# Token embedding, sink attention and soft mixture of experts on one core: two powers in place of four in GpSimd's scale chain

## The chip, the cores and the metric

The kernel runs on one core of a Trainium2 chip. The metric is the device time of one execution in microseconds (us), as the median of several runs; lower is better. An engine is named by its short name in the profile: PE is TensorE (matmul), PEld its weight load, DVE VectorE, ACT ScalarE, POOL GpSimd, SP SyncE. L1104 is line 1104 of the kernel.

## What is computed

For 64 images (3 x 224 x 224) and 64 texts (128 tokens of width 192):

```python
h = tokenize(x)                      # 196 patches per image, layernorm over 3840 values, times W
h = concat([h, txt], axis=1)         # 324 tokens of width 192
h = h + attention(layernorm(h))      # 12 heads, causal, rotary, one sink logit a head, softmax
h = h + experts(layernorm(h))        # soft mixture of 64 slots
```

The part that the change touches is the head of `experts`. Its input is the second layernorm of h; a root-mean-square norm follows, then a norm to unit length, and the product with the slots gives the logits:

```python
def _layernorm(x):  return (x - m) / jnp.sqrt(v + 1e-5)
xn  = x * jax.lax.rsqrt(ms + 1e-5) * norm_weight        # ms = mean(x * x)
tok = xn / jnp.maximum(jnp.sqrt(jnp.sum(xn * xn)), 1e-5)
logits = einsum('sd,btd->bst', sl, tok)                 # softmax over tokens, and over slots
```

For each token this is one factor for xn (alpha in the kernel) and one for the logits (beta).

## The kernel before, in words

After a short preparation of the weights, the body is a loop over batches b (one image and its text), written as a software pipeline. Each engine has its own function `step(b, i)`, run for b from -3 to 64, and engines meet at semaphores only (`Signal`, whose `wait` takes a batch number). In step b PE does, in an order written out by hand:

- a first loop over the 12 heads: `scores` of head h (the query-key products, L605 and L607), for the row maxima that DVE takes (L961). Between heads stand pieces of other batches: `token_values` and `embed` of coming batches, the logits of batch b-1 (L705, after heads 7 and 8), and after head 8 `maxima(b, 0)` (L674), a transposition of the maxima of heads 0 to 5; after head 10 the transposition of the logits (L719);
- a second loop over the 12 heads: `scores_t` (L624 to L630), the transposed products with the maxima subtracted. The maxima enter as three more rows of the queries, so head 0 waits for `max_in[0]`, a DMA that puts the transposed maxima `mt` into `qst`. ACT takes the exponential of each head (L899, shown as L814, the line of its helper), and `values` (L646) multiplies by the values;
- the end of the step: dispatch of batch b-1, transposition of the normed tokens, `project` (L771), output of the attention (L790, L667, L805).

POOL's step for the same b, in its order: `rest` (L1097), then the chain of **the two factors** for batch b-1 (L1104 to L1124), then `maxima_parts(b, 0)` (L1081 to L1087), which splits the maxima of heads 0 to 5 into three bf16 parts `mpart` for PE's L674, then part 2 of the rotated queries and keys (L1131), `maxima_parts(b, 1)`, the factors of the first norms (L1138 to L1147), and the rotation (L1151, L1152). POOL takes them strictly in this order.

Before the change the chain of the two factors has twelve arithmetic instructions on tiles of 128 x 3 values, four of them powers (`power`, L1074, which also drains POOL first):

```python
alpha = (var + eps) ** -0.5                     # L1104, L1105
pw = (var * alpha**2 + eps) ** -0.5             # L1107 to L1112
alpha = alpha * pw                              # L1114
beta_t = alpha / max(zss ** 0.5 * alpha, 1e-5)  # L1116 to L1124, waits for zs_ready
```

`zss` is the sum of squares of z (the centred tokens times the norm's weight), which ACT makes with three Square instructions (L851) and signals as `zs_ready`. `beta_t` is read by ACT when it copies the logits out of PSUM (L869), `alpha` by DVE in the dispatch (L1025). ACT's order after that: the scaled logits, then the copy of the transposed maxima (`mt<-ps`, L875), then the issue of their DMA (L829), the exponentials of the logits, `dexp` (L888), and the twelve exponentials of the heads.

A second part of the program, after the loop, streams the experts' weights (L1190 and on), and a third mixes the outputs. Neither holds anything that the change edits.

Of the kernel before, what the change touches and what calls it, by code (L numbers as in the profile page):

```python
# [24 lines left out]
ALU = mybir.AluOpType  # L25
# [16 lines left out]
EPS = 1e-5  # L42
# [33 lines left out]
def early_fusion_kernel(nc, x, txt, gamma, beta, W, bias, nscale, nbias, Wa, ba, Wproj, bp, sinks, rezero, slots, scale,  # L76
# [8 lines left out]
    with ExitStack() as ctx:  # L85
# [7 lines left out]
        with ExitStack() as layers:  # L93
# [16 lines left out]
            with ExitStack() as work:  # L110
                def tmp(name, shape, dt=F32):
                    return work.enter_context(nc.sbuf_tensor(name, shape, dt))
# [193 lines left out]
            with ExitStack() as work:  # L306
# [39 lines left out]
                bn, mv1, mv2 = tmp("bn", [128, 3, 6]), tmp("mv1", [128, 3, 2]), tmp("mv2", [128, 3, 2])  # L346
                bn2 = tmp("bn2", [128, 3, 6])
                rstd2 = tmp("rstd2", [128, 3])
                zss, alpha, beta_t = tmp("zss", [128, 3]), tmp("alpha", [128, 3]), tmp("beta_t", [128, 3])
                pw = tmp("pw", [128, 3])  # L350
                neg_half, pos_half, neg_one, eps = (tmp(n, [128, 3]) for n in ("neg_half", "pos_half", "neg_one", "eps"))
                zero = tmp("zero", [128, 3, NH // 2])

                logit, lexp = tmp("logit", [128, 3, NS]), tmp("lexp", [128, 3, NS])
# [70 lines left out]
                with nc.Block() as block:  # L425
                    @block.vector
                    def _(dve):
                        for i in range(2):

                            dve.memset(kst[i][SINK_ROW:128], 1.0)  # L430
                            dve.memset(kst[i][0:SINK_ROW, :, KEYS:3 * 128], 0.0)
                            dve.memset(kst[i][0:SINK_ROW, :, 0:1], 0.0)
                            dve.memset(vaug[i][:], 0.0)
                        for t in (xw, xt, *h_new, mv1, mv2, negmax, zss, stat1):
                            dve.memset(t[:], 0.0)
                        dve.memset(neg_half[:], -0.5)
                        dve.memset(eps[:], EPS)
                        dve.memset(zero[:], 0.0)
                        dve.memset(per_strip[:], 1.0 / STRIP)
                        dve.memset(pos_half[:], 0.5)  # L440
                        dve.memset(neg_one[:], -1.0)
                        for t in (lmax, lsum, mrest, rstd2):
                            dve.memset(t[:], 1.0)
                        dve.drain()
                        for i in range(2):
                            dve.memset(vaug[i][:, :, :, HD:HD + 1], 1.0)
                            dve.memset(kst[i][SINK_ROW:MAX_ROW], 0.0)
                        dve.memset(xt[HALF:HALF + 1, 0, 1:KEYS], 1.0)
                        dve.drain().then_inc(prepared, 1)

                    @block.gpsimd
                    def _(pool):
                        for i in range(2):
                            pool.drain()
                            pool.memset(qst[i][SINK_ROW:128], 1.0)
                        pool.drain()
                        pool.memset(yt[HALF:HALF + 1, 0], 1.0)
                        pool.drain()
                        pool.memset(y_all[HALF:HALF + 1, 0], 1.0)

                    @block.sync
                    def _(sp):
                        sp.wait_ge(prepared, 1)
                        for i in range(2):
                            sp.dma_start(kst[i][SINK_ROW:MAX_ROW, :, 0:1], sink_p[:],
                                         allow_slow_non_contiguous=True).then_inc(sinks_in, 16)
                        sp.wait_ge(sinks_in, 32)
# [6 lines left out]
                def has(batch):  # L474

                    return not isinstance(batch, int) or 0 <= batch < B
# [594 lines left out]
                def _(pool):  # L1071
                    def power(dst, src, e):
                        pool.drain()
                        return pool.tensor_tensor(dst, src, e, ALU.pow)  # L1074
# [16 lines left out]
                    def step(b, i):  # L1091
                        moe, att, front, mid = has(b - 1), has(b), has(b + 2), has(b + 1)
                        if mid:

                            for side in range(2):
                                p1_ready.wait(pool, b + 1, side + 1)
                                pool.tensor_tensor(rest[:, side], rot[:, side], part[0][:, side], ALU.subtract  # L1097
                                                   ).then_inc(rest_ready.sem, 1)
                        if moe:

                            ln2_ready.wait(pool, b - 1)
                            dp_ready.wait(pool, b - 2)
                            var = mv2[:, :, 1]
                            pool.tensor_tensor(alpha[:], var, eps[:], ALU.add)  # L1104
                            power(alpha[:], alpha[:], neg_half[:])  # L1105
                            pool.drain()
                            pool.tensor_tensor(pw[:], alpha[:], alpha[:], ALU.mult)  # L1107
                            pool.drain()
                            pool.tensor_tensor(pw[:], var, pw[:], ALU.mult)
                            pool.drain()  # L1110
                            pool.tensor_scalar(pw[:], pw[:], EPS, 1.0, ALU.add, ALU.mult)
                            power(pw[:], pw[:], neg_half[:])  # L1112
                            pool.drain()
                            pool.tensor_tensor(alpha[:], alpha[:], pw[:], ALU.mult)  # L1114

                            zs_ready.wait(pool, b - 1, apart=True)  # L1116
                            power(pw[:], zss[:], pos_half[:])
                            pool.drain()
                            pool.tensor_tensor(pw[:], pw[:], alpha[:], ALU.mult)
                            pool.drain()  # L1120
                            pool.tensor_scalar(pw[:], pw[:], 1e-5, 0.0, ALU.max, ALU.add)
                            power(pw[:], pw[:], neg_one[:])
                            pool.drain()
                            pool.tensor_tensor(beta_t[:], pw[:], alpha[:], ALU.mult).then_inc(beta_ready.sem, 1)  # L1124
                        if att:
                            maxima_parts(b, 0)
                        if mid:
                            stack_in.wait(pool, b)
                            for side in range(2):
                                p2_ready.wait(pool, b + 1, side + 1)  # L1130
                                pool.tensor_tensor(part[2][:, side], rest[:, side], part[1][:, side], ALU.subtract  # L1131
                                                   ).then_inc(p3_ready.sem, 1)
                        if att:
                            maxima_parts(b, 1)
                        if front:

                            stat_ready.wait(pool, b + 2)
                            pool.tensor_tensor(rstd1[:], stat1[:, 0:2], stat1[:, 0:2], ALU.mult)  # L1138
                            pool.drain()
                            pool.tensor_tensor(rstd1[:], stat1[:, 2:4], rstd1[:], ALU.subtract)  # L1140
                            pool.drain()
                            pool.tensor_scalar(rstd1[:], rstd1[:], 0.0, EPS, ALU.max, ALU.add)
                            power(rstd1[:], rstd1[:], neg_half[0:TILE, 0:2]).then_inc(rstd1_ready.sem, 1)

                            ln1_ready.wait(pool, b + 2)
                            pool.tensor_tensor(rstd2[:], mv1[:, :, 1], eps[:], ALU.add)
                            power(rstd2[:], rstd2[:], neg_half[:]).then_inc(rstd2_ready.sem, 1)  # L1147

                            for side in range(2):
                                rope_ready.wait(pool, b + 2, side + 1)  # L1150
                                pool.tensor_tensor(rot[:, side, 0], by_cos[:, side, 0], by_sin[:, side, 1], ALU.subtract)  # L1151
                                pool.tensor_tensor(rot[:, side, 1], by_sin[:, side, 0], by_cos[:, side, 1], ALU.add  # L1152
                                                   ).then_inc(rot_ready.sem, 1)

                    run(step, pool)


# [255 lines left out]
```

## Time and profile before

| | us |
|---|---|
| median of 3 runs | 3242.63 |
| lowest and highest run | 3231.22, 3243.88 |
| the profiled execution, its own time | 3236.77 |
| span of the profiled execution | 3235.0 |
| busy in it: PE | 2841.3 (88%) |
| PEld | 2110.1 (65%) |
| DVE | 1649.1 (51%) |
| ACT | 1607.5 (50%) |
| POOL | 1214.2 (38%) |
| in POOL, four powers of the chain (L1074), 64 of each | 75.2 + 54.5 + 54.5 + 55.1 |

The span runs from the first instruction to the last. The loop over batches fills it from about 190 to 2765 us; the experts follow to about 3100, the mixing to the end. A row of busy time tells what an engine did, not what waited for it; the rows of waits and the timelines tell that. In a timeline each row has start in us, length in us, engine, line, operation, output and inputs, and in brackets how long the engine had been idle and what ended the idle time.

### The profile page before, as it was taken

The numbers are of one execution on the slowest core, as the hardware profiler recorded it, in microseconds if no ns is written. First come the engines' busy times: TensorE is split into PE (matmuls) and PEld (weight loads), VectorE is DVE, ScalarE is ACT, GpSimd is POOL, SyncE is SP. The second block draws the span as 40 slices with busy tenths as digits, with TensorE's granted clock in tenths as the row PEclk, the third lists the DMA queues.
The fourth block names the chain that finished last, engine by engine and source line by source line (L and its number), as shares of the span: only waits on it lengthen the run. The fifth ranks groups of instructions, "written<-read, shape, count | busy, mean of one in ns | idle before, by whom it ended". The sixth has DMA issues, their size and how long they took to land. (4 is left out here: it accounts for less than half of the span.)

```text
span 3235.0 us, 74217 instructions
## 1 busy us (share of the span) xinstructions
PE 2841.3 (88%) x27010; PEld 2110.1 (65%) x27010; DVE 1649.1 (51%) x5416; ACT 1607.5 (50%) x3234; POOL 1214.2 (38%) x2197
## 2 busy tenths in 40 slices
PE   3079999999999999999999999999999998677765
PEld 3057777777777777777777777777777776343432
DVE  2435556556665655555555556555555554111123
ACT  0036666666666666666666666666666654100000
POOL 2134444444444444444444444444444442000000
PEclk8589999999999999999999999999999998788878
DMA  4233333333333333333333333333333321899979
GB/s 107 44 94 89 89 89 89 89 89 90 92 95 91 95 90 94 90 91 90 93 91 90 93 91 92 90 91 91 89 89 89 89 73 36 220 270 234 250 217 290
DMA packets 368824, 361.31 MB, mean 112 GB/s; under 512 B 32478, under 2 KB 339755, under 8 KB 368204
## 3 DMA queue, kind: packets, MB, share of 16 engines
q1 hardware_dynamic: 344332, 339.13, 40.2%
q10 hardware_dynamic: 24128, 17.42, 1.7%
q8 instruction: 216, 3.54, 0.5%
q14 instruction: 148, 1.21, 0.1%
HBM read 196.51 MB, written 43.25 MB: 74 GB/s over the span
## 5 line engine op out<-in xcount | busy, mean ns | idle before, releaser
L961 DVE TENSOR_REDUCE negmax<-ps 128x1 f32<-128x325 f32 (+2 forms) x2304 | 668.2, 350 | 154.6 <-PE ps L607 147.9
L562 PE MATMUL ps<-window_w,xp 108*98 108x193 f32 x2304 | 505.5, 338 | 107.7 <-ACT xp L814 107.7
L814 ACT ACTIVATE prob<-ps 128x590 f32<-128x590 f32 x768 | 500.8, 660 | 180.2 <-PE ps L630 165.2
L605 PE MATMUL ps<-kst,qst 99*128 99x325 bf16 (+2 forms) x2304 | 397.1, 252 | 22.2 <-DVE negmax L961 22.1
L562 PEld LDWEIGHTS ps<-window_w,xp 108*98 108x98 f32 x2304 | 337.2, 166 | 110.7 <-ACT xp L814 107.8
L1151 POOL TENSOR_TENSOR rot<-by_cos,by_sin 96x324 f32<-96x324 f32 x128 | 111.8, 873 | 684.3 <-DVE by_sin L1054 684.3
L607 PE MATMUL ps<-causal,ident_b 128*128 128x128 bf16 (+1 forms) x2304 | 336.0, 214 | 0.0
L771 PE MATMUL ps<-xt,wqk 97*96 97x324 f32 (+1 forms) x1024 | 320.9, 446 | 1.7 <-ACT xt L814 1.7
L605 PEld LDWEIGHTS ps<-kst,qst 99*128 99x128 bf16 (+1 forms) x2304 | 225.2, 104 | 120.3 <-DVE negmax L961 40.1
L646 PE MATMUL ps<-prob,vaug 128*32 128x324 f32 (+2 forms) x4608 | 285.6, 340 | 0.0
L1041 DVE RECIPROCAL rden<-ps 98x12 f32<-98x12 f32 (+1 forms) x192 | 43.4, 226 | 384.0 <-PE ps L790 383.9
L624 PE MATMUL ps<-qst,kst 102*128 102x295 bf16 x768 | 228.1, 297 | 2.8 <-ACT prob L814 1.5
L814 ACT ACTIVATE xp<-xw 108x1764 f32<-108x1764 f32 x64 | 220.0, 3438 | 8.4 <-DMA xw<-in_x_dram 8.4
L607 PEld LDWEIGHTS ps<-causal,ident_b 128*128 128x128 bf16 (+1 forms) x2304 | 204.9, 104 | 21.5 <-issue 0.2
L771 PEld LDWEIGHTS ps<-xt,wqk 97*96 97x96 f32 (+1 forms) x1024 | 157.8, 165 | 83.3 <-issue 5.1
L1254 PE MATMUL ps<-w,y_all 97*64 97x384 f32 (+1 forms) x512 | 127.0, 655 | 82.6 <-DMA w<-in_L_ffn_fc_bias_dram 82.6
L627 PE MATMUL ps<-qst,kst 102*128 102x197 bf16 x768 | 189.5, 247 | 0.0
L1131 POOL TENSOR_TENSOR part<-by_cos,part 96x648 bf16<-96x648 f32 x128 | 178.1, 1411 | 15.5 <-DMA qst<-part 13.2
L1097 POOL TENSOR_TENSOR by_cos<-rot,part 96x648 f32<-96x648 f32 x128 | 178.4, 1415 | 0.0
L1312 ACT ACTIVATE hidden<-ps 128x768 f32<-128x768 f32 x32 | 26.0, 811 | 292.3 <-PE ps L1254 292.3
L625 PE MATMUL ps<-ident_b,causal 128*128 128x127 bf16 x768 | 170.7, 222 | 0.0
L628 PE MATMUL ps<-ident_b,causal 128*128 128x128 bf16 x768 | 170.2, 222 | 0.0
(184 smaller groups left out, 5884.1 us busy)
## 6 DMA issues: line engine op xcount, KB each, us to landing
w<-in_L_ffn_fc_weight_dram SPq DMA_DIRECT2D x128, 576.0 KB, 13.2
xw<-in_x_dram SPq DMA_DIRECT2D x384, 189.0 KB
qst<-part SPq DMA_DIRECT2D x768, 60.8 KB
kst<-part SPq DMA_DIRECT2D x768, 60.8 KB
h_held<-h_new SPq DMA_DIRECT2D x64, 288.0 KB, 4.3
residual_image<-h SPq DMA_DIRECT2D x64, 147.0 KB
h_i<-residual_image SPq DMA_DIRECT2D x16, 588.0 KB
out_dram<-h_i ACTq DMA_DIRECT2D x32, 294.0 KB
```

What stands on the lines that cost most here:

```text
L562: mm = pe.matmul(ps[0:TILE, BK7, half * (D + 1):(half + 1) * (D + 1)], xp[:, q, TILE * half:TILE * (half + 1)], window_w[:, q, :], start=( ...
L605: pe.matmul(ps[0:nq, bk, col:col + keys], qst[i][0:MAX_ROW, h, q0:q0 + nq], kst[i][0:MAX_ROW, h, 0:keys], start=True, stop=False)
L607: mm = pe.matmul(ps[0:nq, bk, col + q0 + 1:col + keys], ident_b[:, 0:nq], causal[:, 0:nq], start=False, stop=True)
L624: pe.matmul(ps[:, bank, 0:EXPC], k0, q[:, 0:EXPC], start=True, stop=False)
L625: pe.matmul(ps[:, bank, 0:127], causal[:], ident_b[:, 1:128], start=False, stop=True)
L627: pe.matmul(ps[:, bank + 1, c1:c2], k1, q[:, KTILES[1][2]:T], start=True, stop=False)
L646: mm = pe.matmul(ps[STRIP * s:STRIP * (s + 1), BK6, q0:T], vaug[i][0:nk, k, h, :], prob[0:nk, h % 8, col:col + T - q0], start=(k == 0), st ...
L771: mm = pe.matmul(ps[0:HALF, SC + 2 * side + e, 0:T], wqk[0:k, c, 2 * side + e, :], xt[0:k, c, 1:KEYS], start=(c == 0), stop=(c == 1))
L814: return nc.scalar.activation(out_, in_, f, **kw)
L961: last = dve.tensor_reduce(negmax[0:nq, q, h:h + 1], ps[0:nq, bk, col:col + q0 + nq + 1], AX.X, ALU.max, negate=True)
L1097: pool.tensor_tensor(rest[:, side], rot[:, side], part[0][:, side], ALU.subtract).then_inc(rest_ready.sem, 1)
L1131: pool.tensor_tensor(part[2][:, side], rest[:, side], part[1][:, side], ALU.subtract).then_inc(p3_ready.sem, 1)
```

## The change

The two factors are written in another form. With v the variance and e = 1e-5, the old alpha is (v + e)^-0.5 times (v/(v + e) + e)^-0.5, which is (v(1 + e) + e²)^-0.5; and alpha / max(sqrt(zss) alpha, 1e-5) is alpha times (max(zss alpha², 1e-10))^-0.5. Nothing else is changed, apart from two constant tiles and their memsets that are no longer needed.

```diff
-                neg_half, pos_half, neg_one, eps = (tmp(n, [128, 3]) for n in ("neg_half", "pos_half", "neg_one", "eps"))
+                neg_half, eps = (tmp(n, [128, 3]) for n in ("neg_half", "eps"))
...
-                        dve.memset(pos_half[:], 0.5)
-                        dve.memset(neg_one[:], -1.0)
...
                             ln2_ready.wait(pool, b - 1)
                             dp_ready.wait(pool, b - 2)
-                            var = mv2[:, :, 1]
-                            pool.tensor_tensor(alpha[:], var, eps[:], ALU.add)
+                            pool.tensor_scalar(alpha[:], mv2[:, :, 1], 1.0 + EPS, EPS * EPS, ALU.mult, ALU.add)
                             power(alpha[:], alpha[:], neg_half[:])
                             pool.drain()
                             pool.tensor_tensor(pw[:], alpha[:], alpha[:], ALU.mult)
                             pool.drain()
-                            pool.tensor_tensor(pw[:], var, pw[:], ALU.mult)
+
+                            zs_ready.wait(pool, b - 1, apart=True)
+                            pool.tensor_tensor(pw[:], zss[:], pw[:], ALU.mult)
                             pool.drain()
-                            pool.tensor_scalar(pw[:], pw[:], EPS, 1.0, ALU.add, ALU.mult)
+                            pool.tensor_scalar(pw[:], pw[:], 1e-10, 0.0, ALU.max, ALU.add)
                             power(pw[:], pw[:], neg_half[:])
-                            pool.drain()
-                            pool.tensor_tensor(alpha[:], alpha[:], pw[:], ALU.mult)
-
-                            zs_ready.wait(pool, b - 1, apart=True)
-                            power(pw[:], zss[:], pos_half[:])
-                            pool.drain()
-                            pool.tensor_tensor(pw[:], pw[:], alpha[:], ALU.mult)
-                            pool.drain()
-                            pool.tensor_scalar(pw[:], pw[:], 1e-5, 0.0, ALU.max, ALU.add)
-                            power(pw[:], pw[:], neg_one[:])
                             pool.drain()
                             pool.tensor_tensor(beta_t[:], pw[:], alpha[:], ALU.mult).then_inc(beta_ready.sem, 1)
```

POOL's instructions of one step before the change, from the last `rest` to the first of `maxima_parts(b, 0)`; mv holds mean and variance, negmax the maxima of the scores:

```order
L1104 TENSOR_TENSOR alpha<-mv,eps 128x3 [waits dp_ready,ln2_ready]
L1074 TENSOR_TENSOR alpha<-alpha,neg_half 128x3
L1107 TENSOR_TENSOR pw<-alpha 128x3
L1109 TENSOR_TENSOR pw<-mv,pw 128x3
L1111 TENSOR_SCALAR pw<-pw 128x3
L1074 TENSOR_TENSOR pw<-pw,neg_half 128x3
L1114 TENSOR_TENSOR alpha<-alpha,pw 128x3
L1074 TENSOR_TENSOR pw<-zss,pos_half 128x3 [waits zs_ready,prepared]
L1119 TENSOR_TENSOR pw<-pw,alpha 128x3
L1121 TENSOR_SCALAR pw<-pw 128x3
L1074 TENSOR_TENSOR pw<-pw,neg_one 128x3
L1124 TENSOR_TENSOR beta_t<-pw,alpha 128x3
```

The same place of the changed kernel, whose lines are numbered anew (L1072 is the power, L1079 the first of `maxima_parts`):

```order
L1101 TENSOR_SCALAR alpha<-mv 128x3 [waits dp_ready,ln2_ready]
L1072 TENSOR_TENSOR alpha<-alpha,neg_half 128x3
L1104 TENSOR_TENSOR pw<-alpha 128x3
L1108 TENSOR_TENSOR pw<-zss,pw 128x3 [waits zs_ready,prepared]
L1110 TENSOR_SCALAR pw<-pw 128x3
L1072 TENSOR_TENSOR pw<-pw,neg_half 128x3
L1113 TENSOR_TENSOR beta_t<-pw,alpha 128x3
L1079 TENSOR_TENSOR mpart<-negmax,zero 128x3x6 [waits mt_mm,max_ready]
```

Twelve instructions have become seven, and the wait for `zs_ready` stands ahead of the fourth in place of the eighth. PE, ACT and SP keep their instructions in their order; DVE loses two memsets in the preparation.

## Rows read from the trace of the kernel before

**Rows 1.** Busy times by stretch (us; count; TensorE clock; DMA share, GB/s)

```profile
1500.00:1900.00 400.00, 387.37 (x3966) 298.62 (x3965) 236.68 (x818) 249.18 (x504) 185.48 (x343) 1.00 0.35 91
```

**Rows 2.** Waits over the whole span: us in total, times, longest

```profile
PE ps L674 <- POOL mpart L1087: 49.4, 62, 1.2
```

**Rows 3.** Timeline of POOL in one step, from the chain to the first maxima

```profile
1564.94 0.30 POOL L1104 TENSOR_TENSOR alpha<-mv,eps 128x3 f32<-128x3 f32 x1
1565.39 1.18 POOL L1074 TENSOR_TENSOR alpha<-alpha,neg_half 128x3 f32<-128x3 f32 x1
1566.72 0.19 POOL L1107 TENSOR_TENSOR pw<-alpha 128x3 f32<-128x3 f32 x1
1567.05 0.19 POOL L1109 TENSOR_TENSOR pw<-mv,pw 128x3 f32<-128x3 f32 x1
...
1570.43 0.24 POOL L1121 TENSOR_SCALAR pw<-pw 128x3 f32<-128x3 f32 x1 [0.16 <-issue]
1570.82 0.86 POOL L1074 TENSOR_TENSOR pw<-pw,neg_one 128x3 f32<-128x3 f32 x1
...
1571.98 0.23 POOL L1081 TENSOR_TENSOR mpart<-negmax,zero 128x18 bf16<-128x18 f32 x1
...
1573.05 0.22 POOL L1087 TENSOR_TENSOR mpart<-mrest,mpart 128x18 bf16<-128x18 f32 x1
```

**Rows 4.** Timeline of DVE in the same step, the maxima of heads 5 and 6

```profile
1568.58 1.88 DVE L961 TENSOR_REDUCE negmax<-ps 128x1 f32<-128x325 f32 x6 [0.20 <-PE ps L607]
```

**Rows 5.** Timeline of PE in the same step

```profile
1572.13 0.56 PE L705 MATMUL ps<-slots_t,zt 96*128 96x64 f32 x4
1573.42 0.30 PE L674 MATMUL ps<-ident_b,mpart 68*18 68x68 bf16 x3 [0.74 <-POOL mpart L1087]
...
1575.23 0.31 PE L605 MATMUL ps<-kst,qst 99*128 99x325 bf16 x1 [0.30 <-DVE negmax L961]
...
1577.00 0.29 PE L624 MATMUL ps<-qst,kst 102*128 102x295 bf16 x1
...
1577.80 0.29 PE L624 MATMUL ps<-qst,kst 102*128 102x295 bf16 x1
...
1578.76 0.30 PE L624 MATMUL ps<-qst,kst 102*128 102x295 bf16 x1
```

**Rows 6.** Timeline of ACT in the same step

```profile
1567.21 0.19 ACT L814 ACTIVATION_READ_ACCUMULATOR lexp<-z 128x1 f32 x1
...
1572.72 0.73 ACT L814 ACTIVATE logit<-ps,beta_t 98x64 f32<-98x64 f32 x3 [0.78 <-PE ps L705]
1573.76 0.43 ACT L814 ACTIVATE mt<-ps 18x324 bf16<-18x324 bf16 x1 [0.32 <-PE ps L674]
1574.22 0.76 ACTq L829 DMA_DIRECT2D qst<-mt  x1
...
1578.07 2.00 ACT L814 ACTIVATE prob<-ps 128x590 f32<-128x590 f32 x3
```

**Rows 7.** DMA queues from the issue on: 1.90 and 2.00 us, same step

```profile
q10 hardware_dynamic: 20, 0.01, 2.1%
...
q10 hardware_dynamic: 21, 0.01, 2.0%
```

**Rows 8.** DMA queues of the earlier step, 2.40 us from the issue on

```profile
q10 hardware_dynamic: 21, 0.01, 1.7%
```

**Rows 9.** Weight loads of L624 and the DMA's issue: the same step, and an earlier one

```profile
1576.84 0.10 PEld L624 LDWEIGHTS ps<-qst,kst 102*128 102x128 bf16 x1
...
1216.16 0.75 ACTq L829 DMA_DIRECT2D qst<-mt  x1
...
1219.15 0.10 PEld L624 LDWEIGHTS ps<-qst,kst 102*128 102x128 bf16 x1 [0.38 <-DMA qst<-mt]
```

**Rows 10.** ACT and PE after the loop's last step

```profile
2757.37 0.72 ACT L814 ACTIVATE logit<-ps,beta_t 98x64 f32<-98x64 f32 x3 [3.52 <-POOL beta_t L1124]
...
2753.90 2.45 PE L705 MATMUL ps<-slots_t,zt 96*98 96x64 f32 x12 [0.87 <-ACT zt L814]
```

## The prediction

> **What bounds the kernel now.** I read the busy times by stretch first. In the middle of the loop over batches PE is busy 387.4 of 400 us at a granted clock of 1.00 (the 2.4 GHz level), POOL 185.5 [rows 1]. So PE sets the pace and POOL's own load costs nothing; POOL can only matter where PE waits for it. Second, the list of waits: PE waited for POOL's last instruction on `mpart` 62 times, 49.4 us in all, 0.80 us each in the mean and at most 1.2 [rows 2]. That is once in each full step, and it is the one thing the change can give back. The timelines of one step say why. POOL runs the chain of the two factors without a pause from 1564.94, and its next instruction, the first of `maxima_parts`, starts at 1571.98 right behind it [rows 3]. That instruction wanted nothing later: the maxima of heads 5 and 6 are taken in one run from 1568.58 to 1570.46, so head 5's were there by about 1569.5 [rows 4]. The last `mpart` ends at 1573.27 [rows 3] and PE's L674 starts at 1573.42 after 0.74 us of idleness [rows 5]. The wait is POOL's place in the queue, not its data.
>
> **The chain on POOL.** Before, from the chain's start to `maxima_parts`: 1571.98 - 1564.94 = 7.04 us for twelve instructions [rows 3]. After, seven, priced by the pitch (start to start, drains included) of their nearest rows. The first becomes a tensor_scalar; a tensor_scalar's pitch is 0.39 (1570.43 to 1570.82) and the old first one's 0.45, stretched beside DVE's work; I take 0.45, bounds 0.34 and 0.6, since the same DVE work lies beside it. The power 1.33 (to 1566.72), the square 0.33 (to 1567.05). This comes to 1567.05. Then the wait for `zs_ready`, which now stands earlier in the chain: ACT's last accumulator read ends at 1567.21 + 0.19 = 1567.40 [rows 6], so POOL stands still for about 0.4 us, and nothing but `maxima_parts` is queued behind it. From 1567.45: product 0.33, tensor_scalar 0.39, power and last product 1.16 (1570.82 to 1571.98) give 1569.33. So `maxima_parts` can start at about 1569.35, 2.65 us earlier; it waits then for head 5's maxima, to 1569.55, and its four instructions take 1573.27 - 1571.98 = 1.29, to 1570.85. The power with exponent -1 takes 0.86, the one beside DVE's work 1.18 [rows 3]; both kept powers have exponent -0.5, and I take the second at the pitch of the former.
>
> **What of it reaches PE.** PE comes to L674 behind the logits' product L705, 0.56 us long from 1572.13, without a wait at about 1572.62 (matmuls start some 0.07 before the modelled end of the last). `mpart` is there 1.8 us before. L674 starts 0.80 us earlier in this step, 0.06 more than the idle time shown. In the mean of all 62 steps that is 0.80 + 0.06 = 0.86 at most. Everything up to head 11's scores follows: they waited 0.30 for DVE's maxima of head 9 [rows 5], whose scores stand right behind L674 and move with it.
>
> **Where the wait goes.** The second loop's first product, L624 of head 0, needs the DMA that puts the transposed maxima into the queries. Its source is the copy `mt` on ACT, at 1573.76 after 0.32 us of waiting for L674. But ACT takes the scaled logits first, 1572.72 to 1573.45, released by PE's L705 (0.78 <-PE), not by beta [rows 6]; the change doesn't move them. So the copy moves by 0.36 at most, to 1573.40, and the issue of the DMA from 1574.22 to 1573.86. How long does the DMA take? In the same step its packets (21) were all taken between 1.90 and 2.00 us after the issue [rows 7]. What comes behind the last packet is read in a step where PE did wait: issued 1216.16, all packets by 2.40 us [rows 8], L624's weights at 1219.15, 2.99 after the issue [rows 9]. That gives some 0.6 behind the last packet, so 2.5 to 2.6 in the step at hand. The room was 1576.84 - 1574.22 = 2.62 [rows 9]: the DMA arrived just in time. With PE 0.80 earlier it is late. L624's weights come at 1573.86 + 2.5 = 1576.36, a gain of 0.48, not 0.80. Bounds of the landing: 2.2, where the gain is whole, and 2.99, where it is nothing (-0.01).
>
> Part of the rest comes back two heads later. Head 2's L624 started at 1578.76; heads 0 and 1 are 0.80 apart, so PE alone would have been there at 1578.60, and the difference was a wait for ACT's exponential of head 0. ACT's exponentials start at 1578.07 without idle time [rows 6], behind `dexp` and so behind DVE's maxima, which move by the full 0.80, to 1577.27. That wait of 0.16 is gone. So the gain from head 2 on is 0.48 + 0.16 = 0.64 in this step (landing 2.4: 0.74; 2.6: 0.54). From there the step is PE's. `maxima_parts(b, 1)` waits for DVE and moves with it. Part 2 of the rotated tensors comes some 2 us earlier on POOL; the only DMAs that wait for it stand at the end of SP's step behind all others, so this brings nothing, and costs nothing if I am wrong, since it is earlier.
>
> The Trainium skill (DMA: Bandwidth & Descriptors, "Anatomy of one DMA — SWDGE (gpsimd) path") puts a DMA at about 2.0 us plus its bytes over 436 GB/s, and says that most of the 2.0 lies behind the last byte. For the few KB here my estimate from that page is 2.0 us; it was fitted for the other issue path. By it the DMA would not bind at all and the sum below would be 54 instead of 44. The trace has packets still being taken at 1.90 and does not agree, so I go by the rows.
>
> **The sum.** The step at hand has an idle time of 0.74, the mean is 0.80; the longer ones gain the excess in ACT's copy as well. So 0.64 + 0.06 = 0.70 a step, times 62 = 43.4 us. After the last step the logits on ACT start at 2757.37, released by beta after 3.52 us; PE's L705 was done at 2753.90 + 2.45 = 2756.35 [rows 10]. POOL's chain is over 1 us shorter there too, so PE takes over: 2757.37 - 2756.4 = 0.9 us. Two memsets less on DVE are under 0.2 us beside loads, nothing. Together 44.3 us. The weights' streaming behind the loop is as long as before and starts earlier.
>
> From the profiled execution's own 3236.8 that gives 3192.5. The median of the runs shown is 5.9 above it and would give 3198.3. I take the middle, 3195. About 0.5%, 16 us, is what a measurement of this kernel can tell from no change.
>
> **The rivals.**
> 1. *The whole wait goes* (chance 0.22). If the DMA lands 2.2 us or less after its issue, the mechanism being a receipt that is quicker than the 0.6 I read in one step, PE keeps 0.86 a step: 62 x 0.86 + 0.9 = 54.2, 3182 to 3188. For it: in the step at hand the DMA made PE wait for nothing, so 2.5 to 2.6 is where it may be at the latest, not where it must be. Against: it did wait in some, with up to 2.99. This is the case that the skill's 2.0 us would make.
> 2. *The DMA takes back more* (0.13). Landing 2.6 and more: only ACT's 0.36 and a part of the longer waits count, about 0.42 a step, 27 us, 3210 to 3216.
> 3. *No change* (0.09). `maxima_parts` starts where it did, because something else held it: `mt_mm` of the step before, or the maxima. Against it: no idle time ahead of 1571.98. Or the steps' pace is set elsewhere, by ACT or SP, and PE only waits later: 3237 to 3243.
> 4. *Slower* (0.04). The DMA is issued 0.36 us earlier among SP's `qst<-part` and `kst<-part` DMAs, and may get in their way so that it lands later than it gained. It decides from a landing of 2.99 us on; 3.3 in the mean would cost 0.3 a step, 62 x 0.3 = 19 us, 3256 to 3262. The longest that I read is 2.99, with most far below, so this is unlikely.
>
> **How the numbers follow.** Forecast 0.52. The cases 1 and 2 are also faster by over 16 us, so faster has 0.52 + 0.22 + 0.13 = 0.87, same 0.09, slower 0.04. The range takes in the forecast and the case on either side of it, with the base's uncertainty (3231 to 3244 in the runs): 3178 to 3218, which leaves out cases 3 and 4 and the edges of the others.
>
> **What would show it.** POOL: seven instructions from `rest` to `maxima_parts`, about 4.6 us, with a wait of 0.4 for ACT ahead of the product with zss, and one of 0.2 for DVE ahead of `mpart`. PE: the wait of L674 for POOL gone from the list of waits. PEld: L624 of head 0 waits for the DMA `qst<-mt` in most steps, 0.1 to 0.5 us. The step's period shorter by 0.7. The forecast is wrong if the DMA wait does not appear and the period is shorter by 0.8 or more (case 1), or if PE's wait for `mpart` stays.

## The result, and the profile after

The changed kernel took 3183.20 us in the median of four runs (3179.41 to 3188.93), the kernel before 3243.26 (3231.22 to 3248.11, four runs). The ratio is 0.983, 95% interval 0.9804 to 0.9856: faster by 1.7%, 60 us. A later pair on another chip gave 0.9868 (0.9832 to 0.9905).

First the waits of the whole span of the changed kernel (total us, times, longest), whose lines are numbered anew: L672 is the old L674, L622 the old L624, L603 the old L605.

```profile
POOL mpart L1079 <- DVE negmax L959: 143.4, 67, 6.9
...
PEld ps L622 <- DMA qst<-mt: 52.6, 94, 1.4
...
POOL pw L1108 <- ACT lexp L812: 41.9, 64, 1.6
...
PEld ps L603 <- DVE negmax L959: 32.1, 77, 2.4
...
PE ps L603 <- DVE negmax L959: 13.8, 72, 2.2
...
PE ps L622 <- DMA qst<-mt: 7.9, 20, 1.2
```

The same waits in the kernel before:

```profile
POOL mpart L1081 <- DVE negmax L961: 66.7, 65, 5.7
...
PEld ps L624 <- DMA qst<-mt: 37.3, 70, 1.1
...
PE ps L624 <- DMA qst<-mt: 0.8, 2, 0.5
```

The row of [rows 2], PE's wait for `mpart`, is gone from the list. POOL now waits for the sum of squares (L1108), where it did not. Its wait for the maxima has grown from 66.7 to 143.4 us, and that is the second group of a step, `maxima_parts(b, 1)`, which POOL now reaches earlier: 2.16 us in the step below, 0.91 in the step of [rows 3].

The row of the DMA needs to be taken apart, since each step has two such DMAs. The second, for heads 6 to 11, is waited for by a weight load in each of the 64 steps, 35.5 us in all before and 35.9 after, so the change has nothing to do with it. The first, which head 0 needs, was waited for in 6 steps (1.8 us) and is waited for in 30 now (16.7 us). PE's own wait has gone from 0.8 to 7.9 us.

One step on POOL, in the form of [rows 3]:

```profile
1539.50 0.20 POOL L1101 TENSOR_SCALAR alpha<-mv 128x3 f32<-128x3 f32 x1
1539.85 1.16 POOL L1072 TENSOR_TENSOR alpha<-alpha,neg_half 128x3 f32<-128x3 f32 x1
1541.15 0.19 POOL L1104 TENSOR_TENSOR pw<-alpha 128x3 f32<-128x3 f32 x1
1541.97 0.20 POOL L1108 TENSOR_TENSOR pw<-zss,pw 128x3 f32<-128x3 f32 x1 [0.63 <-ACT lexp L812]
1542.32 0.25 POOL L1110 TENSOR_SCALAR pw<-pw 128x3 f32<-128x3 f32 x1 [0.16 <-issue]
1542.72 0.86 POOL L1072 TENSOR_TENSOR pw<-pw,neg_half 128x3 f32<-128x3 f32 x1
1543.72 0.19 POOL L1113 TENSOR_TENSOR beta_t<-pw,alpha 128x3 f32<-128x3 f32 x1
1544.00 0.22 POOL L1079 TENSOR_TENSOR mpart<-negmax,zero 128x18 bf16<-128x18 f32 x1
...
1545.07 0.22 POOL L1085 TENSOR_TENSOR mpart<-mrest,mpart 128x18 bf16<-128x18 f32 x1
```

`mpart` is there at 1545.29. PE asks for it 1.8 us later and starts without idle time, where it had sat idle for 0.74 us in [rows 5]:

```profile
1546.56 0.56 PE L703 MATMUL ps<-slots_t,zt 96*128 96x64 f32 x4
1547.05 0.31 PE L672 MATMUL ps<-ident_b,mpart 68*18 68x68 bf16 x3
```

ACT in the same step, to be held against [rows 6], and the weight load that the DMA releases, to be held against [rows 9]:

```profile
1547.16 0.72 ACT L812 ACTIVATE logit<-ps,beta_t 98x64 f32<-98x64 f32 x3 [0.78 <-PE ps L703]
1547.76 0.41 ACT L812 ACTIVATE mt<-ps 18x324 bf16<-18x324 bf16 x1
1548.20 0.76 ACTq L827 DMA_DIRECT2D qst<-mt  x1
```

```profile
1550.47 0.10 PEld L622 LDWEIGHTS ps<-qst,kst 102*128 102x128 bf16 x1
...
1552.40 0.10 PEld L622 LDWEIGHTS ps<-qst,kst 102*128 102x128 bf16 x1 [0.31 <-ACT prob L812]
```

The copy `mt` has lost its wait and follows the scaled logits at once. From the issue to the weight load it is 2.27 us where it was 2.62; I call this time the room. The second line is the weight load of head 2, which waits 0.31 us for an exponential on ACT, as it did before:

```profile
1578.76 0.10 PEld L624 LDWEIGHTS ps<-qst,kst 102*128 102x128 bf16 x1 [0.31 <-ACT prob L814]
```

How much of the 60 us lies in the loop over batches is read from its last instruction, ACT's last write of `y_all` (minimum, median and maximum ns, then first and last start). Before and after:

```profile
L814 ACT ACTIVATE y_all<-ps x64: 381/387/394, 282.1 to 2765.1; 96x128 f32<-96x128 f32 x64
```

```profile
L812 ACT ACTIVATE y_all<-ps x64: 380/387/394, 279.7 to 2715.8; 96x128 f32<-96x128 f32 x64
```

The loop ends 49.3 us earlier. The part behind it takes 3235.0 - 2765.1 = 469.9 us before and 3177.6 - 2715.8 = 461.8 after. That difference is not the change's: in a second profile of the same changed kernel it is 469.9, and over all the profiles of this study, none of which edits that part, it lies between 443 and 478. So I use the loop's end as the measure below: it is 2714.7 in the second profile of the changed kernel, 1.1 us from the first. It has some chance in it too: the preparation ahead of the loop, where the change leaves out two memsets and nothing else, lets the first write of `y_all` start anywhere from 279.7 to 282.9 us in these profiles, so a difference of 3 us between two loop ends says nothing by itself. The 1.7% of the first comparison is the loop's 49 us (1.5%) and some 10 us of chance.

### The profile page after: what moved, and what is told of

It reads as the page before. It is cut to its first block and busy times, and to the rows that moved or that the text cites. A ratio compares the mean times of both kernels' runs of the same rounds, so it can differ in the third digit from the quotient of the medians.

```text
span 3177.6 us, 73575 instructions
## 1 busy us (share of the span) xinstructions
PE 2842.1 (89%) x27010; PEld 2102.9 (66%) x27010; DVE 1651.1 (52%) x5414; ACT 1602.7 (50%) x3234; POOL 1064.2 (33%) x1877
## 3 DMA queue, kind: packets, MB, share of 16 engines
q14 instruction: 142, 1.16, 0.1%
## 5 line engine op out<-in xcount | busy, mean ns | idle before, releaser
L603 PE MATMUL ps<-kst,qst 99*128 99x325 bf16 (+2 forms) x2304 | 394.9, 251 | 13.8 <-DVE negmax L959 13.8
L605 PE MATMUL ps<-causal,ident_b 128*128 128x128 bf16 (+1 forms) x2304 | 334.0, 213 | 0.0
L603 PEld LDWEIGHTS ps<-kst,qst 99*128 99x128 bf16 (+1 forms) x2304 | 224.3, 104 | 111.5 <-issue 38.7
L1039 DVE RECIPROCAL rden<-ps 98x12 f32<-98x12 f32 (+1 forms) x192 | 43.4, 226 | 385.3 <-PE ps L788 385.3
L622 PE MATMUL ps<-qst,kst 102*128 102x295 bf16 x768 | 227.8, 297 | 10.9 <-DMA qst<-mt 7.9
L605 PEld LDWEIGHTS ps<-causal,ident_b 128*128 128x128 bf16 (+1 forms) x2304 | 204.0, 103 | 21.6 <-issue 0.2
L1120 POOL TENSOR_TENSOR part<-by_cos,part 96x648 bf16<-96x648 f32 x128 | 178.1, 1411 | 36.9 <-ACT part L812 35.5
L622 PEld LDWEIGHTS ps<-qst,kst 102*128 102x128 bf16 x768 | 77.8, 101 | 139.9 <-issue 53.7
```

The costliest lines, as they stand in the source:

```text
L603: pe.matmul(ps[0:nq, bk, col:col + keys], qst[i][0:MAX_ROW, h, q0:q0 + nq], kst[i][0:MAX_ROW, h, 0:keys], start=True, stop=False)
L605: mm = pe.matmul(ps[0:nq, bk, col + q0 + 1:col + keys], ident_b[:, 0:nq], causal[:, 0:nq], start=False, stop=True)
L622: pe.matmul(ps[:, bank, 0:EXPC], k0, q[:, 0:EXPC], start=True, stop=False)
```

## The experiments

Every kernel was run against the kernel before on its own chip; the ratio's 95% interval is in brackets. Theory 1 is the prediction's: PE waited because `maxima_parts` stood behind the long chain on POOL, and what is gained there is limited by the DMA of the maxima.

| kernel | ratio | loop ends at | PE's wait for `mpart`, us |
|---|---|---|---|
| before | 1 | 2765.1 | 49.4 |
| the change | 0.9830 (0.9804 to 0.9856) | 2715.8 | none |
| alpha_only | 0.9818 (0.9785 to 0.9852) | 2713.1 | 0.7 |
| beta_only | 0.9870 (0.9844 to 0.9896) | 2726.8 | 7.1 |
| pad1 | 0.9796 (0.9760 to 0.9832) | 2715.3 | 0.6 |
| pad2 | 0.9899 (0.9875 to 0.9924) | 2726.7 | 13.1 |
| pad3 | 1.0226 (1.0197 to 1.0255) | 2841.3 | 79.5 |
| before_h9 | 0.9893 (0.9869 to 0.9916) | 2734.1 | 23.7 |
| late_dma | 0.9845 (0.9828 to 0.9862) | 2721.0 | none |
| mt_dve | 0.9851 (0.9822 to 0.9879) | 2711.5 | none |
| change_again | 0.9868 (0.9832 to 0.9905) | 2714.7 | none |
| mt_dve_again | 0.9867 (0.9827 to 0.9907) | 2707.2 | none |

**alpha_only: one half of the rewriting.** Against the changed kernel:

```diff
                             power(alpha[:], alpha[:], neg_half[:])
                             pool.drain()
-                            pool.tensor_tensor(pw[:], alpha[:], alpha[:], ALU.mult)
-                            pool.drain()
                             zs_ready.wait(pool, b - 1, apart=True)
-                            pool.tensor_tensor(pw[:], zss[:], pw[:], ALU.mult)
+                            power(pw[:], zss[:], pos_half[:])
+                            pool.drain()
+                            pool.tensor_tensor(pw[:], pw[:], alpha[:], ALU.mult)
                             pool.drain()
-                            pool.tensor_scalar(pw[:], pw[:], 1e-10, 0.0, ALU.max, ALU.add)
-                            power(pw[:], pw[:], neg_half[:])
+                            pool.tensor_scalar(pw[:], pw[:], 1e-5, 0.0, ALU.max, ALU.add)
+                            power(pw[:], pw[:], neg_one[:])
```

> Only the layernorm's half of the rewriting is made (three powers are left, nine instructions and eight after them none). Theory 1, POOL's place in the queue: the chain ends about 1.1 us later than with both halves, mpart is ready at about 0.8 us before PE asks for it, so PE does not wait and the time is that of the full change, 3180 to 3190 us. Theory 2, each power taken away gives its own share: half of the gain, about 3213 us.

It took 3181.35 us and its loop ended at 2713.1, the whole gain. The chain has one power more than with the full change, and the slack swallows it: counted from the chain's start, `mpart` ends at 6.74 us in place of 5.79, and PE waits in one step only. Theory 2, by which each removed power pays its share, falls.

**beta_only: the other half.** The first part of the chain is as before, four instructions longer:

```diff
-                            pool.tensor_scalar(alpha[:], mv2[:, :, 1], 1.0 + EPS, EPS * EPS, ALU.mult, ALU.add)
+                            var = mv2[:, :, 1]
+                            pool.tensor_tensor(alpha[:], var, eps[:], ALU.add)
                             power(alpha[:], alpha[:], neg_half[:])
...
+                            pool.tensor_tensor(pw[:], var, pw[:], ALU.mult)
+                            pool.drain()
+                            pool.tensor_scalar(pw[:], pw[:], EPS, 1.0, ALU.add, ALU.mult)
+                            power(pw[:], pw[:], neg_half[:])
+                            pool.drain()
+                            pool.tensor_tensor(alpha[:], alpha[:], pw[:], ALU.mult)
+                            pool.drain()
+                            pool.tensor_tensor(pw[:], alpha[:], alpha[:], ALU.mult)
```

> Only the logits' half is made (three powers, eleven instructions). Theory 1: mpart ends 2.0 us later than with both halves, which is 0.1 to 0.3 us after PE asks for it; PE waits for POOL by that much in each of 62 steps, partly in place of its wait for the DMA: 3186 to 3200 us. Theory 2, shares: about 3213 us.

3194.75 us, loop end 2726.8: 38.3 of the 49.3 us. The two halves alone give 52.0 and 38.3, together 49.3. They are not additive: what the second half would add lies beyond the point where the wait is gone. PE's own row shows only 7.1 us in 14 steps; the rest is in the weight loads' idle time ahead of L672:

```profile
PEld ps L672 <- issue: 36.2, 125, 1.9
...
PE ps L672 <- POOL mpart L1085: 7.1, 14, 1.8
```

That first row is 15.8 in 63 times with the full change. The difference, 20 us over 62 steps, is 0.33 us a step, of which 0.18 is lost in the loop.

**pad1, pad2, pad3: the changed kernel with needless powers ahead of `maxima_parts`.** The text is that of pad3; the others repeat once and twice.

```diff
                             pool.tensor_tensor(beta_t[:], pw[:], alpha[:], ALU.mult).then_inc(beta_ready.sem, 1)
+                            for _ in range(3):
+                                power(pad[:], eps[:], neg_half[:])
```

> The full change, and one needless power of 1.0 us on POOL between beta and the first maxima (the result is not used). Theory 1: POOL has 1.65 us of slack there, nothing changes: 3180 to 3190 us. Theory 2 (POOL's busy time itself costs): 62 us more, 3245 us; a share of POOL's work through its contention with VectorE would give 3190 to 3200 us.

> The full change, with two needless powers (2.0 us) ahead of the first maxima. With none and with one PE doesn't wait and the loop ends at 2715; with three it waits 1.28 us a step and the clock falls to 0.97 or 0.98 for much of the loop (2841). Here the wait is 0.3 to 0.4 us a step: 15 to 22 us more, loop end 2730 to 2740, and the granted clock stays at 1.00. If the clock is lost with any wait, it shows 0.99 or less and the loop ends past 2760.

> The full change, and three needless powers (3.0 us) at the same place. Theory 1: the slack of 1.65 us is used up, PE waits 1.3 us in each of 62 steps, 80 us more, less what it waited for the DMA (15 us): 3245 to 3260 us, slower than the kernel before by 0.2 to 0.3 us a step. Theory 2, each power 62 us: 3370 us. Theory 3, the gain came from fewer powers beside VectorE's work and not from the wait: about 3240 us at most, with no wait of PE for POOL in the list.

A needless power of 1.0 us on POOL in each step costs nothing (2715.3 against 2715.8), two cost 10.9 us, three 125.5. Neither POOL's busy time nor its contention with DVE is what the change saved; its place in the queue is. pad1 and pad2 fit theory 1 in kind. pad1's median of 3172.53 us lies below the expected 3180 to 3190, and its part behind the loop was the shortest of all, 443.0 us. pad2 stayed below its range: PE waits 0.21 us a step (expected 0.3 to 0.4), and the loop ends 10.9 us later, at 2726.7 (expected 15 to 22, at 2730 to 2740). pad3 came out far beyond its range of 3245 to 3260, at 3310. The wait itself was as expected, 79.5 us in 63 steps:

```profile
PE ps L672 <- POOL mpart L1085: 79.5, 63, 2.9
```

The rest is the clock. Four stretches of 4 us in one step of pad3, around the wait (span of the stretch; PE, PEld, DVE, ACT, POOL busy with counts; granted clock; DMA share and GB/s):

```profile
1572.00:1576.00 4.00, 3.45 (x42) 2.69 (x39) 2.94 (x10) 2.11 (x6) 3.22 (x7) 1.00 0.75 203
1576.00:1580.00 4.00, 2.76 (x26) 2.19 (x27) 2.20 (x9) 1.58 (x9) 3.14 (x4) 0.83 0.37 98
1580.00:1584.00 4.00, 4.00 (x30) 3.42 (x29) 1.04 (x4) 1.89 (x6) 0.87 (x4) 0.74 0.35 88
1584.00:1588.00 4.00, 4.00 (x50) 2.90 (x48) 1.49 (x8) 2.78 (x5) 0.39 (x2) 1.00 0.39 103
```

```profile
1576.94 0.30 PE L672 MATMUL ps<-ident_b,mpart 68*18 68x68 bf16 x3 [1.50 <-POOL mpart L1085]
```

PE had been idle for 1.50 us, to 1576.94. The granted clock then falls to 0.83 and 0.74 in two stretches, so for a part of them to the lower of its two levels (1.2 and 2.4 GHz), though PE is busy again throughout the second. Over the middle of the loop:

```profile
300.00:2400.00 2100.00, 2013.64 (x20097) 1559.78 (x20093) 1206.29 (x4155) 1270.35 (x2568) 959.02 (x1647) 0.97 0.34 88
```

The same stretch has 1.00 with the kernel before, with the change and with pad1 (pad1's has 21205 matmuls in it, against 20097). So 125.5 us are 79.5 of waiting, and the remaining 46 stand beside a clock of 0.97. Taken step by step, from one wait to the next, the two come apart. In 25 steps the trace shows no stretch at the lower clock, and they last 40.0 to 40.7 us, the 38.75 of the changed kernel plus one wait. In 36 it shows such a stretch, and they last 40.9 to 42.4 us, 1.26 us more in the mean. 36 times 1.26 is 45 us, which is the rest. The waits in most steps of both kinds are of the same length, 1.20 to 1.22 us, so what decides between them is not the length alone and stays open. Waits of 0.74 us, once a step, had cost no clock in the kernel before.

**before_h9: another way to take the wait from PE.** The kernel before, all four powers kept:

```diff
-                            if att and h == 8:
+                            if att and h == 9:
                                 v_ready.wait(pe, b + 1, apart=True)
                                 mpart_ready.wait(pe, b, 1)
                                 maxima(b, 0)
```

> The kernel before, with all four powers; only PE's transposition of the first six maxima is moved from behind head 8's scores to behind head 9's, so that PE works 0.42 us in place of waiting. The copy on ScalarE and its DMA cannot start earlier than before, since mpart comes when it came. PE reaches the second loop 0.4 to 0.6 us earlier a step, with a room of 2.0 to 2.2 us for the DMA in place of 2.62. If the DMA takes 2.2 to 2.3 us from its issue in most steps (theory 1, corrected after the result), the gain is about 0.35 to 0.5 us a step, 3210 to 3218 us, and the loop ends at 2734 to 2743. If it takes 2.5 to 2.6 us as the prediction had it, the gain is 0.07 to 0.25, 3222 to 3233 us.

The loop ends at 2734.1, 31.0 us earlier than before, 0.50 us a step. POOL has not changed by an instruction, and six tenths of the change's gain are there. The DMA is now late:

```profile
PEld ps L624 <- DMA qst<-mt: 65.8, 124, 1.6
...
PE ps L674 <- POOL mpart L1087: 23.7, 62, 2.0
PE ps L624 <- DMA qst<-mt: 12.3, 35, 1.4
```

Since the weight load of head 0 waits for it in nearly every step (60 of 64), the time from the issue on ACT to that load is the DMA's own: 2.05 us at the shortest, 2.42 in the median, 3.05 at the longest. So the corrected guess of 2.2 to 2.3 in the expectation was too short for the median and the prediction's 2.5 to 2.6 too long. The time came out at the good end all the same: 0.50 us a step and a loop end of 2734.1, where 2734 to 2743 was expected, and a median of 3201.54, below the expected 3210 to 3218. The next run shows why a DMA of 2.4 us costs so little.

**late_dma: the DMA a third of a microsecond later in the changed kernel.**

```diff
+                        if g == 0:
+                            fn(late[:], ident[:, 0:64], ACT.Copy)
+                            act.drain()
                         act.dma_start(qst[i][MAX_ROW:STACK, NH // 2 * g:NH // 2 * (g + 1), :], mt[g][:]
```

> The full change, with one needless copy of 128 x 64 values on ScalarE, and a drain, between the transposed maxima of group 0 and the issue of their DMA, 0.3 to 0.5 us. The room between issue and first use falls from 2.27 to under 2.0 us, so PE's weight load waits in every step and each step shows how long the DMA takes. Corrected theory 1: median 2.2 to 2.3 us, loop 15 to 30 us longer. The prediction's step: 2.5 to 2.6 us in the median. If the DMA is no gate at all (rival: another signal releases PE), the loop keeps its length and no wait for the DMA appears.

The issue comes 0.31 us later (0.75 us after the start of the copy `mt`, 0.44 without the edit), PE's weight load waits in 58 of 64 steps, and the time from the issue is 2.04 to 2.99 us with a median of 2.51. By this run's own test that is the prediction's figure and not the corrected one. Yet the loop is only 5.2 us longer, 0.08 us a step, where 15 to 30 us were expected. The reason is in the waits for ACT: the weight loads' wait for the exponential of an earlier head (`PEld ps L622 <- ACT prob`) falls from 13.9 us to 5.4. What the DMA delays at head 0 would have been waited for at head 2.

How much of a delay is free can be read from the change alone, step by step. In 24 of its 64 steps the weight load stands 2.27 to 2.29 us after the issue, so the DMA was in time. In 30 it waits for the DMA, up to 3.19 us after the issue, and in the other 10 it starts later without a wait that the profile marks (it marks none under 0.15 us). The time from one issue to the next is 38.75 us where the load was in time, and still 38.75 to 38.8 in nearly all steps where it came up to 2.6 us after the issue. Beyond that the step grows by what the DMA is late: 39.03 us at 2.85, 39.36 at 3.19. So the first 0.3 us cost nothing, which is the 0.31 us that head 2 waits for ACT in any case, and only the late tail of the DMA costs time. What all steps last beyond 38.75 us comes to 8.5 us in this profile and 7.0 in the second one, nearly all of it in steps with a late DMA.

**mt_dve: a version that starts the DMA earlier.** In the changed kernel DVE, idle for 0.6 us there, makes the copy in place of ACT:

```diff
                                 last.then_inc(max_ready.sem, 1)
+                            if att and h == 8:
+                                mt_mm.wait(dve, b, 1)
+                                max_in[0].wait(dve, b - 1)
+                                dve.tensor_copy(mt[0][:], ps[0:PARTS * NH // 2, BK6, :].bitcast(BF16)[:, 0:T]
+                                    ).then_inc(mt_ready[0].sem, 1)
...
-                            fn(mt[0][:], ps[0:PARTS * NH // 2, BK6, :].bitcast(BF16)[:, 0:T], ACT.Copy
-                                ).then_inc(mt_ready[0].sem, 1)
```

> The full change, and the copy of the transposed maxima of group 0 is made by VectorE, idle there for 0.6 us, in place of ScalarE, which still issues the DMA behind its scaled logits. The issue comes about 0.3 us earlier, the room grows from 2.27 to 2.5 to 2.6 us, and most of what PE still waits for this DMA (15 steps or so with 0.3 to 0.9 us, 15 us of the weight loads' idle time) goes: loop 5 to 12 us shorter than with the change alone, about 3173 to 3178 us. If the DMA waits are only late DMAs that come late whatever the issue, nothing changes.

```profile
PEld ps L603 <- DVE negmax L955: 40.6, 77, 1.8
...
PEld ps L622 <- DMA qst<-mt: 38.3, 75, 1.0
...
PE ps L603 <- DVE negmax L955: 22.2, 72, 1.5
...
PE ps L622 <- DMA qst<-mt: 1.1, 3, 0.8
```

The room grows to 2.73 us (expected 2.5 to 2.6), and the wait for the DMA of head 0 is left in 11 steps of 64, where it was in 30: 4.3 us of the weight loads' time in place of 16.7. The waits for DVE's maxima, which come earlier in the step, have risen by 8.5 us in the weight loads and 8.4 in PE.

The loop ended at 2711.5, 4.3 us before the change's, a little under the 5 to 12 expected. To see whether that lasts, both were run again on one chip:

> The change itself once more, on the same chip as the next kernel, as the measure for it. The loop over batches ends at 2712 to 2718 us in its profile (2715.8 the first time); its DMA of the transposed maxima is waited for in 20 to 30 of 57 steps. The part behind the loop, 443 to 471 us in the profiles so far, decides the rest: 3175 to 3190 us.

> The copy of the transposed maxima on VectorE, once more. Its loop ended 4.3 us before that of the change. If that is real, the loop ends at 2709 to 2713 us again and the median is 0 to 8 us below the change on the same chip; if the first reading was chance, the two loops end within 2 us of each other.

The loops ended at 2714.7 and 2707.2 (expected for the latter 2709 to 2713). From the first write of `y_all` to the last, which leaves out the preparation, mt_dve is shorter by 6.5 us in the first pair and 7.9 in the second, so the copy on DVE is worth some 7 us of the loop. The medians were 3184.75 and 3182.79 us, with ratios of 0.9868 and 0.9867. In the time of the whole kernel nothing can be told apart, since the part behind the loop varies by more. mt_dve is no worse than the change, and in the time of the whole kernel it is not shown to be better.

## Why the prediction was right

**The bound.** PE's wait for POOL, once a step and 49.4 us in all, was the thing to be given back, and it is gone. pad1 and before_h9 show that it was the order on POOL: the powers may stay if PE does not ask so early, and POOL may be busy if the work stands in slack.

**The chain on POOL.** Forecast: 4.6 us from the end of `rest` to `maxima_parts`, measured 1544.00 - 1539.42 = 4.58; from the chain's start it is 4.50, to be held against 7.04 before. The wait ahead of the product with zss is 0.63 us where I had 0.4: the instructions ahead took 0.13 less than taken, and the 0.63 begins at the end of the square where my sum had added its drain, 0.14, first. The forecast wait of 0.2 for DVE ahead of `mpart` is too short for the profile to mark; the product ahead of it takes 0.28 to the next start, and 0.16 in alpha_only, where the maxima had been there for longer. PE has `mpart` 1.8 us ahead of its need, as forecast.

**PE up to the DMA.** L674 was to start 0.80 us earlier, right behind L705. It does, at 1547.05, 0.49 after the start of L703 (forecast 1572.62 - 1572.13 = 0.49).

**The DMA.** The forecast that it would take back a part was right: PE's waits for it rose by 7.1 us and the weight loads' by 15.3. Its size in the sum was nearly right as well, 0.86 - 0.70 = 0.16 us a step or 9.9 us, where what the steps last beyond 38.75 us comes to 8.5 and 7.0 us in the two profiles. But that is in part luck, for the working behind it has three pieces that are off. The issue on ACT was said to move by 0.36 us; measured from L705's start it moved by 2.09 - 1.64 = 0.45, because the copy, no longer waiting, starts before the end that the profile gives for the scaled logits. What comes back at head 2 was taken as 0.16 us, from the distance of PE's starts; the weight load's own row has 0.31. With these two a landing of 2.5 us in every step would have cost nothing: late by 2.5 - 2.27 = 0.23, and 0.31 is free. And the landing was taken as 2.5 us for every step, from the packets of one step and the tail of another, where it spreads from 2.04 to 3.19 in the three kernels read; the steps beyond some 2.6 are the ones that cost.

**The loop.** Its gain was forecast as 44.3 us and measured as 49.3. From the issue of the first step to that of the last, 63 steps, it is 47.1 us or 0.75 a step (forecast 43.4, 0.70 a step). The changed kernel was 1.6 us ahead at the first issue already (0.7 in its second profile), which is chance, and the end brought 0.6. The signs named beforehand are mixed: the step's period is shorter by 0.80 in the median (39.55 to 38.75) and 0.75 in the mean, where 0.7 was forecast, and the waits for the DMA are there, but in 30 steps of 64 and not in most. The gain lies in the middle between the forecast and rival 1, and the median of 3183.2 us even inside rival 1's 3182 to 3188. Its reason, a DMA that lands within 2.2 us, is refuted all the same: it can take 3.2.

**The end of the loop.** Forecast 0.9 us from the last logits. They are released by PE's L703 now, no longer by beta, and ACT's idle time ahead of them has gone from 3.52 to 2.54 us:

```profile
2708.08 0.72 ACT L812 ACTIVATE logit<-ps,beta_t 98x64 f32<-98x64 f32 x3 [2.54 <-PE ps L703]
```

**The total.** 3195 forecast, 3183.2 measured, inside the range of 3178 to 3218. Of the 12 us between them 5 are the loop's. The others are in no term of the sum: the part behind the loop was shorter by 8.1 us in the profiled execution by chance, the base was put 2.5 above the profiled execution, and the median of the changed kernel is 3.8 above its own profiled execution (5.0 + 8.1 + 2.5 - 3.8 = 11.8). I gave the base an uncertainty and that part none of its own, though it streams weights over DMA and is the least steady part of the kernel.

**The rivals.** No change (3) is refuted by the list of waits, slower (4) by the result: the earlier issue loses 0.1 us a step and not more than it gained. pad3 was slower, but by another way, a wait of PE for POOL of 1.2 us and more.

## What to carry to other kernels

An engine at 38% can hold up one at 88% by the order of its queue alone: look for the wait whose releaser starts its work straight behind something unrelated, and ask how much of that something must go until the wait is nought. Beyond that point more savings buy nothing (one power fewer or two gave the same here), and the next gate, here a small DMA with a room of 2.3 us, takes its part. Where a DMA stands in such a place, read its time as a distribution over all steps, not from one, and look for the wait behind it, which hides the first part of any delay (0.3 us here). Starting it earlier brought some 7 us of the loop (mt_dve); whether it can be made shorter was not tried.

## What the runs showed of the hardware

A wait of 1.2 to 1.5 us of PE in each step of about 40 us was followed by a stretch at the lower clock in 36 of 61 steps, lowered the granted clock to 0.97 over the loop and cost some 45 us on top of the 79.5 us of waiting (pad3). Waits of 0.2 us (pad2) and 0.8 us in the mean (before) left it at 1.00. A DMA of 11.4 KB from ACT, SBUF to SBUF, beside SP's queue at a third of the DMA engines' time, took 2.04 to 3.19 us from issue to the waiting weight load in before_h9, late_dma and the changed kernel, with a median of 2.4 to 2.5 in the first two, though its form and size never change. The longest of all profiles is 3.81 (one step of pad1). A power on 128 x 3 values takes POOL 0.85 to 0.88 us with exponents of 0.5, -0.5 and -1 alike (the first of the chain 1.16 to 1.19), four times a product (0.19). From start to start with the drain it is 1.0 against 0.35, so in this chain a power costs as much as three products.
